# A gated cross-attention block on one core: the query sums come from TensorE as a 113th column, and row statistics and the third value piece change slots

## The reference

```python
x = x + tanh(g_xattn) * xattn(layernorm(x), ctx, ctx)
x = x + tanh(g_ffn) * ffn(layernorm(x))

# xattn: 16 heads of 16
Q, K, V = linear(query), linear(key), linear(value)
qk = einsum('bhqd,bhkd->bhqk', Q, K)
scores = qk / 4
feats = [scores.mean over queries and keys, scores.max(keys).mean(), var(softmax(scores)).mean()]
t = exp(clip(mlp_with_two_gelus(feats)))          # one temperature per batch and head
attn = softmax(qk / (2 t));  out = linear(attn @ V)

# ffn: weights quantised to three levels, activations to 8 bits, silu(gate) * up, down
```

## Time and profile before

| what | value |
|---|---|
| time before, median of 3 runs | 841.13 us (837.73 to 844.13) |
| the profiled execution | 837.44 us, of which the profile's span is 835.6 us |
| TensorE clock granted, mean | 0.961 of full speed |
| busy: PE, DVE, ACT, POOL | 715.0, 725.1, 706.3, 513.7 us |

### The profile page before, as it was taken

The page is one execution under the profiler, slowest core; times in us unless marked ns, Lnnn a source line. Parts: engine busy times, 40 slices in busy tenths (PEclk is TensorE's granted clock), DMA queues, the critical chain, the costliest instruction groups (busy, mean ns, idle before and its releaser), DMA issues.

```text
span 835.6 us, 21360 instructions
## 1 busy us (share of the span) xinstructions
PE 715.0 (86%) x7333; PEld 486.1 (58%) x7346; DVE 725.1 (87%) x1501; ACT 706.3 (85%) x1449; POOL 513.7 (61%) x983
## 2 busy tenths in 40 slices
PE   6555798989999898989898989899997877688896
PEld 5333465666666666666666666666665555345454
DVE  5788898989889898989898989898998877679996
ACT  1577689998999989899999999989899897587896
POOL 4748755666676666766667666666652245446664
PEclk8666899999999999999999999999999999999999
DMA  9997766564667554665656464747461132122222
GB/s 207 194 269 152 149 121 121 114 130 128 146 123 141 120 136 118 143 124 127 126 139 125 124 126 121 144 119 143 111 129 27 51 101 63 49 82 64 77 83 76
DMA packets 119320, 101.18 MB, mean 121 GB/s; under 512 B 27423, under 2 KB 115615, under 8 KB 119199
## 3 DMA queue, kind: packets, MB, share of 16 engines
q1 hardware_dynamic: 115646, 97.78, 51.7%
q10 hardware_dynamic: 3568, 2.04, 1.3%
HBM read 49.54 MB, written 12.85 MB: 75 GB/s over the span
## 4 chain that ended last, share of the span: by engine, by line
PE 36%; ACT 29%; DVE 15%; issue 9%; POOL 4%; DMA 3%; SPq 2%; ACTq 0%; DVEq 0%; POOLq 0%
ACT ex L1101 11%; ACT pt L1091 9%; PE p_o L1234 7%; PE p_m L1327 6%; PE p_s L1217 5%; PE p_m L1300 3%; PE p_t L1255 3%; DVE stats L834 3%; ACT L1091 2%; DVE kst L960 2%; DVE hmax L963 2%; ACT L1119 2%; PE p_m L1316 2%; PE p_m L1310 2%; DVE nm L853 2%
## 5 line engine op out<-in xcount | busy, mean ns | idle before, releaser
L1101 ACT ACTIVATE ex<-p_s,nm 112x375 f32<-112x375 f32 x512 | 271.1, 600 | 11.8 <-DVE nm L853 11.6
L834 DVE BATCH_NORM_STATS2 stats<-ex 112x6 f32<-112x375 f32 x512 | 252.7, 535 | 32.5 <-ACT ex L1101 31.5
L1091 ACT ACTIVATE pt<-p_t,ct 128x336 f32<-128x336 f32 x488 | 241.2, 557 | 38.8 <-PE p_t L1255 37.4
L853 DVE TENSOR_REDUCE nm<-p_s 112x2 f32<-112x750 f32 x256 | 235.8, 922 | 4.4 <-PE p_s L1217 4.3
L1217 PE MATMUL p_s<-kst,qst 96*112 96x375 bf16 x512 | 134.6, 346 | 31.0 <-ACT ex L1101 24.3
L1255 PE MATMUL p_t<-qst,kst 99*128 99x112 bf16 x1464 | 116.9, 213 | 10.6 <-ACT pt L1091 8.4
L1255 PEld LDWEIGHTS p_t<-qst,kst 99*128 99x128 bf16 x1464 | 93.3, 98 | 55.1 <-ACT pt L1091 18.0
L1310 PE MATMUL p_m<-wv_sb,ctxt 128*128 128x256 f32 (+1 forms) x384 | 106.6, 400 | 9.4 <-DVE va L789 5.8
L1234 PE MATMUL p_o<-pt,va 128*32 128x112 f32 (+1 forms) x3072 | 101.6, 265 | 0.5 <-ACT ex L1101 0.5
L1327 PE MATMUL p_m<-ctxt,wk_sb 128*128 128x375 f32 x240 | 93.0, 511 | 0.3 <-DVE qf L802 0.2
L1234 PEld LDWEIGHTS p_o<-pt,va 128*32 128x32 f32 (+1 forms) x3072 | 70.3, 110 | 35.8 <-issue 29.4
(11 more groups left out here) (179 smaller groups left out, 1257.5 us busy)
## 6 DMA issues: line engine op xcount, KB each, us to landing
kst<-kp SPq DMA_DIRECT2D x378, 93.8 KB, 3.4
ctxt<-ctxt_dram SPq DMA_DIRECT2D x32, 375.0 KB, 4.3
qbounce<-qp SPq DMA_DIRECT2D x32, 168.0 KB, 2.5
qst<-qbounce SPq DMA_DIRECT2D x32, 168.0 KB, 3.4
qst<-qbounce SPq DMA_DIRECT2D x32, 112.0 KB, 3.4
xm<-x_dram SPq DMA_DIRECT2D x32, 112.0 KB, 2.4
x_dram<-x SPq DMA_DIRECT2D x32, 112.0 KB, 1.9
xt<-x_dram SPq DMA_DIRECT2D x28, 128.0 KB, 2.9
```

Source lines behind the costliest of these rows:

```text
L834: last = nc.vector.bn_stats(stats[:, nb % RING, 2 * pb + i], ex[0:SQ, 2 * (t % 2) + i, :])
L853: nc.vector.tensor_reduce(nm[:, n % RING, 2 * p:2 * p + 2], p_s[t % 2][0:SQ, :, 0:SK], axis=AX.X, op=ALU.max, negate=True).then_inc(s_max, 1)
L1091: nc.scalar.activation(pt[:, (2 * r + i) % 8], st_home(r, i)[:, 0:KC * SQ].rearrange("k (c q) -> k c q", c=KC), ACT.Exp, scale=ct[:, nr % ...
L1101: last = nc.scalar.activation(ex[0:SQ, 2 * ((t - 1) % 2) + i, :], p_s[(t - 1) % 2][0:SQ, i, 0:SK], ACT.Exp, bias=nm[:, ne % RING, h:h + 1])
```

## The change

1. **The sum of the queries.** `identx` is the 112 x 112 identity with a 113th column of ones. PE no longer transposes `xn` but multiplies it with `identx`, so column 113 of `xnt` is the sum of the rows. The query projection, its copy to `qf` and the copy to `xnt` carry 113 columns. Column 113 of `qf` is the sum without 111 biases; a small addition of `bqs` (111 times the bias) gives `sumq`. It stands on POOL inside `split_q` (for the first batch on DVE). The reduction on DVE and its wait are gone.
2. **Row statistics.** For tiles due up to step 32, `bn_stats` and `bn_aggr` of the second layer norm stand together in place 7 of the even step (two tiles at a time), no longer in places 5 and 6 of every step. SP loads the tiles two slots later. `VAR_AT` and `SQRT_AT` move two slots back.
3. **The third value piece.** In even steps from 2 to 32, DVE's copy of V1 stands at the end of place 7. PE projects V2 at the end of place 7, behind `w3b`, and DVE copies it at the start of place 0 of the odd step. Odd steps into even ones are as before.
4. **Loading.** SP loads `identx` where it loaded `ident`; ACT's queue loads `ident` at t = -2, and DVE makes the bf16 identity at t = 3 and not at t = -6.

```diff
+SX = SQ + 1
...
-        VAR_AT, SQRT_AT, RSTD_AT, RSTD_LATE = SLOTS * B + 6, SLOTS * B + 7, SLOTS * (B + 3) + 2, 18
+        VAR_AT, SQRT_AT, RSTD_AT, RSTD_LATE = SLOTS * B + 8, SLOTS * B + 9, SLOTS * (B + 3) + 2, 18
...
+        def stat_slot(b):
+
+            n = b + P_LAG + 2
+            return SLOTS * n + 5 if n > B else SLOTS * (n + n % 2) + 7
...
-                pool.wait_ge(s_qs, count(1, b, 1))
-                nc.gpsimd.tensor_tensor(qf[:, :, :], qf[:, :, :], hi, ALU.subtract).then_inc(s_qx, 1)
+                nc.gpsimd.tensor_tensor(of, of, hi, ALU.subtract).then_inc(s_qx, 1)
+                nc.gpsimd.tensor_tensor(sumq[:, b % SRING, :], qf[:, :, SQ], bqs[:, :], ALU.add).then_inc(s_qs, 1)
...
-                    if 0 <= n - lag < B:
+                    early = p in (0, 1) and pair_of(n - 1)
+                    if early and p == 0 and 0 <= n - lag < B:
+                        copy_v(n - lag, 2)
+                    elif not early and 0 <= n - lag < B:
                         copy_v(n - lag, ch)
...
-                    nc.vector.tensor_tensor(qf[:, :, :], p_m[:, 0:C * SQ].rearrange("p (c q) -> p c q", c=C),
-                                            bq[:, :].unsqueeze(2).to_broadcast([P, C, SQ]), ALU.add).then_inc(s_qc, 1)
-                    dve.wait_ge(s_qc, count(1, b, 1))
-                    nc.vector.tensor_reduce(sumq[:, b % SRING, :], qf[:, :, :], axis=AX.X, op=ALU.add).then_inc(s_qs, 1)
+                    nc.vector.tensor_tensor(qf[:, :, :], p_m[:, 0:C * SX].rearrange("p (c q) -> p c q", c=C),
+                                            bq[:, :].unsqueeze(2).to_broadcast([P, C, SX]), ALU.add).then_inc(s_qc, 1)
...
+                now = [k for k in range(TILES) if t == stat_slot(need(k))]
+                for k in now:
+                    dve.wait_ge(s_xl2[k % 2], ring_count(16, k, 2))
+                    nc.vector.bn_stats(st2[:, k, :], xt[:, k % 2, :]).then_inc(s_bn2, 1)
+                for k in now:
+                    dve.wait_ge(s_bn2, k + 1)
+                    nc.vector.bn_aggr(mv2[:, k], st2[:, k]).then_inc(s_ag, 1)
+                if p == 7 and pair_of(n) and 0 <= n - V_LAG < B:
+                    copy_v(n - V_LAG, 1)
...
-                        last = nc.tensor.transpose(ride[t % 2][:, c, :], xn[:, c * P:(c + 1) * P], ident[0:SQ, 0:SQ])
+                        last = nc.tensor.matmul(ridex[t % 2][:, c, :], xn[:, c * P:(c + 1) * P], identx[:, :], start=True, stop=True)
...
+                if p == 7 and pair_of(n) and active("V2", n + 1):
+                    value(2, n + 1 - V_AT[0][1], n + 1)
```

More of the change, by code:

```diff
@@ L183, in gated_block @@
         ride = [p_s[i][:, :, RIDE:RIDE + SQ] for i in range(2)]
+        ridex = [p_s[i][:, :, RIDE:RIDE + SX] for i in range(2)]
         o_acc = p_o[:, 0:H // 4 * SQ].rearrange("p (g q) -> p g q", q=SQ)
@@ L359, in _ @@
             load_ctx(0)
-            sp.dma_start(ident[:, :], cst["ident"]).then_inc(s_k, 16)
+            sp.dma_start(identx[:, :], cst["identx"]).then_inc(s_k, 16)
             load_x(1)
@@ L461, in slot @@
                     sp.dma_start(kst[t - ROWS_AT + 1][MROW:MROW + PARTS], kst[0][MROW:MROW + PARTS]).then_inc(s_ones, 16)
[L462 to L471, removed]
+                for k in range(TILES):
+                    if t == stat_load_slot(need(k)):
+                        b = need(k)
+                        sp.wait_ge(s_x2d[b % 2], ring_count(16, b, 2))
+                        if k >= 2:
+                            sp.wait_ge(s_bn2, count(1, k - 2, 1))
+                        else:
+                            sp.wait_ge(s_pbn, PAIRS)
+                        sp.dma_start(xt[:, k % 2, :], x2_rows[P * k:P * (k + 1)]).then_inc(s_xl2[k % 2], 16)
                 i = group_at(t, -3)
@@ L589, in slot @@
                     pool.wait_ge(s_bn, count(SLOTS, n))
+                    pool.wait_ge(s_qs, count(1, n))
                     if j == 1:
@@ L768, in setup @@
                     for i in range(2):
-                        last = nc.vector.bn_aggr(mv[:, b + i], st1[:, b + i])
+                        last = nc.vector.bn_aggr(mv[:, b + i], st1[0:SQ, b + i])
                     last.then_inc(s_pag, 1)
@@ L849, in slot @@
                         dve.wait_ge(s_qmm, count(1, x))
-                    nc.vector.tensor_copy(xnt[:, :, :], ride[t % 2]).then_inc(s_xtc, 1)
+                    nc.vector.tensor_copy(xnt[:, :, :], ridex[t % 2]).then_inc(s_xtc, 1)
                 if 0 <= t < SLOTS * B:
@@ L1012, in slot @@
                 if t == -2:
+                    load(ident, "ident", s_id)
                     for dst, name in ((w2t, "w2t"), (w3b, "w3b"), (b1, "b1"), (b2, "b2"), (b3, "b3"), (hmask, "hmask")):
@@ L1299, in slot, with value @@
                         for k in range(C):
-                            last = mm(p_m[:, c * SQ:(c + 1) * SQ], wq[:, k, c * P:(c + 1) * P], xnt[:, k, :], start=(k == 0), stop=(k == C - 1))
+                            last = mm(p_m[:, c * SX:(c + 1) * SX], wq[:, k, c * P:(c + 1) * P], xnt[:, k, :], start=(k == 0), stop=(k == C - 1))
                     last.then_inc(s_qmm, 1)
-                if p in V_AT and active(f"V{V_AT[p][0]}", n):
-                    ch, lag = V_AT[p]
-                    v = n - lag
-                    take(f"V{ch}", n)
+                def value(ch, v, row):
+                    take(f"V{ch}", row)
                     if v == 0 and ch == 0:
@@ L1311, in slot @@
                     last.then_inc(s_vmm, 1)
+                if p in V_AT and active(f"V{V_AT[p][0]}", n) and not (p == 0 and pair_of(n - 1)):
+                    value(V_AT[p][0], n - V_AT[p][1], n)
                 if p == 3 and active("OP", n):
@@ L1450 @@
         "wgt": np.asarray(L0_ffn_w_gate).T, "wut": np.asarray(L0_ffn_w_up).T, "wdt": np.asarray(L0_ffn_w_down).T,
-        "ident": np.eye(P, dtype=np.float32), "hmask": np.tile(np.eye(HG, dtype=np.float32), (DK, 1)),
+        "ident": np.eye(P, dtype=np.float32), "identx": np.concatenate([np.eye(SQ, dtype=np.float32), np.ones((SQ, 1), np.float32)], axis=1), "hmask": np.tile(np.eye(HG, dtype=np.float32), (DK, 1)),
     }
```

59 lines of the change are left out of this document (27 added, 32 removed).

## The result

The changed kernel takes 850.32 us (median of 4 runs, 849.67 to 851.23) against 839.43 us for the kernel before in the same runs: ratio 1.012, interval 1.009 to 1.015. The forecast was 843. So it is slower by 10.9 us where 2 us were forecast. The profiled execution took 849.67 us, its span is 847.7 us, 12.1 us more than before.

What follows compares the result with a forecast made beforehand. The chain was taken to run through PE and ACT, with DVE busiest but seldom on it. Terms -2.3 + 2.0 + 0.6 + 1.3, plus 0.4 for early steps, gave +2 us: 843 us, range 833 to 851.

Steps and rivals of the forecast that it cites:

- rival 2: The 113-column product on PE does not fit its slack and costs 1.0 us each: 10.5 us, 853 us; chance 0.09.
- Rival 3: V2 on PE comes later than put, K0 0.6 us late instead of 0.15: 6 us, 849 us; chance 0.11.
- V2: DVE's copy heading 13 odd steps makes K0 0.15 us late each: 2.0 us lost, bounds 0 and 3.9.
- the start: Before the steady state, slower fp32 products and additions, less one reduction, on the chain: +0.6 us, bounds 0 and 1.2.
- the end: The later root of the standard deviations takes one more table load on ACT: +1.3 us, bounds 0 and 1.5.
- Slower by over 1%: Whole kernel's time above 849.5 us: chance 0.13.
- signs of being wrong: Steady distance between GELU table loads, forecast 39.5 us: wrong if under 39.2 or above 39.9 us.
- The reduction: Dropping DVE's `sumq` frees 0.42 us a batch, 13.4 us of DVE's time, but 0 on the path.
- Rival 1: DVE is the bound after all, so its relief gets through: 836.6 us, or 832 with even steps; chance 0.18.
- The row statistics: Moving DVE's statistics tiles saves 0.25 us in nine odd steps: 2.3 us gained, bounds 0 and 3.8.
- The ride: PE's 113-column product adds 0.25 us, which fits 0.3 us of slack in even steps: 0 on the path.
- The sum: All terms +1.6 us, plus 0.4 us for early steps: +2 us on a median of 841.13, giving 843 us.

Runs made afterwards that it cites:

- e6: The kernel before with only the query sums changed (ride with 113 columns, addition on POOL, identity loaded later): 844.73 us, ratio 1.0058 to the kernel before.
- e7: The kernel before with only the row statistics moved to place 7, the root as before: 835.84 us, ratio 0.9955 to the kernel before.
- e1: The changed kernel with V2 on PE and its copies on DVE back in their old places: 843.94 us, ratio 1.0046 to the kernel before.
- e5: The kernel before, unchanged, profiled a second time: 838.72 us, ratio 0.999.
- e9: The changed kernel with DVE's copy of V2 behind the statistics of `ex`, V2 on PE still in the GELU slot: 845.18 us, ratio 1.0053.
- e11: The kernel before with two 32-byte gaps that shift kp, qp, kf, qf by 32 bytes and kst by 64, no instruction changed: 842.66 us, ratio 1.002.
- e8: The kernel before with only V2 and its copies moved: 845.9 us, ratio 1.0071 to the kernel before.
- e2: The changed kernel with the variance and root steps two slots earlier again, with the last early tile's statistics: 848.19 us, ratio 1.0102 to the kernel before.
- e10: The changed kernel with V2, its copies and the root as before, plus two 32-byte gaps ahead of kp and behind qf: 841.18 us, ratio 1.0008.

## Why the prediction was right or wrong

The direction was right and the size was not: +10.9 us, forecast +2. The measured 850.32 us lies inside the range of 833 to 851, but by 0.7 us and by luck. The room up there was for rivals 2 and 3, and rival 2 did not come true. In the profiles three terms left their own bounds instead: V2 (4.8 us, bound 3.9), the start (+4.4, bound 1.2) and the end (+5.0, bound 1.5). Slower by over 1%, above 849.5 us, had a chance of 0.13. The signs of being wrong looked at the distance alone: 39.71 us lies between 39.2 and 39.9, and so they stayed silent, while most of the loss was in the start and the end. By its own steps:

- **The reduction, 0 on the path.** Right in sum with the ride: in e6, which has both, the distances stay at 39.33 and 39.59 us, with 386 ns a batch taken from DVE. Rival 1 is out. That one of the two gave something and the other took it is not excluded by a run.
- **The row statistics, -2.3 us.** Right in the distances: e7 and e1 have one distance of 39.32 and 39.35 us for all pairs. With its interval, e7's whole gain is 2.4 to 5.2 us (median 4.0), so the term was, if anything, small; the rest is not settled. The thirteen distances of e7 are 2.3 us shorter than those of e5 and 2.7 us shorter than those of the first profile.
- **The ride, 0.** Right: 0.49 us where 0.5 was forecast, and the 2.31 us around it do not change. In an even step that is 0.29 us more than the transposes' 0.20 us, and the 0.3 us of slack took it whole, barely as forecast. Rival 2 is out.
- **V2, +2.0 us.** The mechanism was right, the size not: K0 is 0.29 us late where 0.15 was put, and itself takes 1.53 for 1.43 us, so that `kf` is 0.39 us late. 13 x 0.37 = 4.8 us, above the bound of 3.9. V2 started 0.33 us behind `w3b` and not 0.25, and DVE's copy began 1.16 us after V2's start, where I had 1.08. Rival 3 held in part, at 0.29 us and not its 0.6; I had carried 0.3 us, for a V2 that waits for the end of `w3b`, as a bound only. The 0.10 us by which K0 itself took longer was in no term; in e9, where K0 is on time, it takes 1.43 us.
- **Start, +0.6 us.** This step failed outright. I counted instructions ahead of the transfers, and these cost nothing in the profile of after (23.84 us against 24.18) and some tenths in others. The 4.4 us (2.4 us against e5) came from transfers that the change does not touch, which its wider tiles had moved in memory. e11 shows that part of the cause in the profile, but not in the times: e6 costs 4.9 us (2.9 to 6.7) and e11 1.7 us (-1.0 to 4.4), which leaves room for some cost of the sums that no profile shows.
- **End, +1.3 us.** Failed as well: +5.0 us in the profiled run. The one load was right (1.28 us). Left out were the 1.09 us for which ACT waits for `vpe`, V2 in the last GELU slot, whose copy stands ahead of the second block's work on DVE (e8, with the old root: 164.9 us against 161.0 to 163.9 in the six profiles with both as before), and the clock. The late root alone (e1) gives 165.0 us, both together 164.9 to 167.6. In all six profiles with the late root the second stretch of 8 us behind the last load has a granted clock of 0.60 to 0.71, in the eight without it 1.00; but four of these eight (e2, e5, e8, e11) have 0.79 in the first. How much of the end is clock was not measured apart, and the two do not go together closely: summed over the end, the clock's shortfall is 6.7 us in e9 (end 167.6 us) and 7.2 us in e11 (162.1 us).
- **The sum** was made against 841.13 us; the kernel before then had 839.43 us in the runs beside the changed one, 1.7 us less.

## What to carry to other kernels

A wait that moves to the head of an engine's list for a step moves all that is queued behind it: put the copy behind the work that is ready, as e9 does, and the same move on PE is free in the steady state. When a change makes a tile wider, compare the addresses of the tiles behind it and the share of the DMA queue for the same bytes, before looking for the cause in the instructions; by the profiles it costs where transfers bound the kernel, here the first 85 us. Parts of a change have signs of their own: run them one by one, since here one of three gained 0.45% inside a change that lost 1.2%.

## What the runs showed of the hardware

- The busy share of the DMA queue for 97.8 MB was 51.0 to 53.5, 59.4 to 60.6 and 67.2 to 68.4% of the span with `kst` at three places 64 bytes apart, the median landing of a 93.8 KB transfer 3.4 to 3.5, 4.0 to 4.1 and 4.7 to 4.8 us, and a packet of 750 bytes 60 to 64, 77 to 79 and 93 to 95 ns. The steady state, bound by PE, ACT and DVE, did not notice: 39.35 us a pair in e1, e9 and e10 alike.
- Within 4 us in which PE was busy for 1.23, the granted clock went from 1.00 to 0.50, and stayed there for some 6 us, the last 3 of them with PE busy throughout. The same four products took 1.97 us there in place of 1.12.
- In even steps two fp32 products by the identity took PE 0.49 us, against 0.20 us for two fp32 transposes; in the odd steps behind a GELU slot 0.44 us (0.54 in e6), against 0.25. That is 1.8 to 2.5 times as long.
